# Conv and attention hybrid, tokens stage: another place in the turn for every kind of piece

## The chip, the cores and the metric

The kernel runs on one core of a Trainium2 chip. The metric is the time of one execution on the device in microseconds (us). The core has a matmul engine (TensorE, PE in the profile), a vector engine (VectorE, DVE), a scalar engine (ScalarE, ACT), GpSimd (POOL) and SyncE (SP), which here issues all of the tokens stage's transfers. Each engine executes its own list of instructions strictly in order; a wait at the head of a list holds up everything behind it. 

## The reference

Input x has shape (32, 96, 56, 56), that is 32 images of 96 channels and 3136 tokens. Cut to what matters:

```python
x = conv3(relu(bn(dwconv(relu(bn(conv1(x))))))) ; x = bn(x) + x_in     # layer 0
t = tokens(x)                                                          # (32, 3136, 96)
h = relu(bn(layernorm(t) @ w1.T))                                      # 192 hidden
X = fft(h, axis=tokens)
xr = relu(X.real * rd - X.imag * idg + rb); xi = relu(X.imag * rd + X.real * idg + ib)
t = t + bn(ifft(xr + 1j * xi).real @ w2.T)
t = t + ffn(layernorm(t))          # 96 -> 384 -> 96, operands rounded to an 8-bit float, sums to 16 bit
```

## The kernel before

Layer 0 takes the first half of the time: its own phases (conv, projection) leave their result for each image in a scratch tensor in HBM. The tokens stage (`tokens_stage`) does the rest, and the change lies wholly in it.

Work of the tokens stage on one image is cut into 40 kinds of pieces, 349 pieces in all. On TensorE: `mean1`, `square1` (sums of layernorm 1, 2 pieces each), `w1` (14), `stage1` (first half of the transform, 14), `spectrum` (second half, 6), `w2` and `stage3` (8 each), `stage4` (7), `mean2`, `square2`, `spread_mean`, `spread_rstd`, `mlp1` (21), `mlp2` (7). The other engines' pieces stand between them: for instance ACT's `act_mean1` (L1504), DVE's `dve_var1` (L1635), ACT's `act_std1` (L1471), and SP's `row1` (L1182), which copies the row of standard deviations with four small transfers into the tile `y`, where `w1` (L1386) takes it as an added row. 

The stage runs as a software pipeline over "turns". A turn has NT = 2000 slots, and `PLACES` gives each piece a place: place % 2000 is its slot in the turn, and place // 2000 is its lag, that is how many images behind the newest one it works. With 32 images and LAGS = 5 there are 36 turns. Every engine walks the slots of a turn in order (`tensor_turn`, `scalar_turn`, `vector_turn`, `pool_turn`, `sync_turn`) and issues its pieces that stand in the slot; pieces of one slot follow in the order in which the function lists them. The slot numbers of different engines are tied by nothing but the semaphores that the pieces wait on: only the order on each engine counts.

Resources that tie pieces together:
- Seven tiles of PSUM. `bank_w` (w1), `bank_s` (stage1), `bank_c` (w2 and stage3) and `bank_o` (stage4 and mlp2) are one bank each and in one copy, so the next piece on it waits until the one before is evacuated: `stage4` c waits for `dve_residual` c-1, `mlp2` c for `act_o` c-1, `w2` u for `dve_c` u-1. `bank_x` (spectrum) is in one copy as well: the next group waits for `dve_real` of the group before. `bank_l0` and `bank_l1` serve both layernorms, the spreads and mlp1.
- One queue of transfers. SP issues `load_in`, `row1`, `store_t`, `store_a`, `load_b`, `store_c`, `load_d`, `load_t`, `store_out` in the order of their slots. The transforms' two transposes go through HBM: `store_a` then `load_b` (L1215, L1192), `store_c` then `load_d` (L1197, L1204). `load_b` k=0 waits for all seven `store_a`; `load_d` k waits for `store_c` k to have landed. `store_c` k waits for `dve_c` of groups 2k and 2k+1. `load_t` brings back the residual tokens of the attention half, chunk by chunk, once `pool_out` has freed the chunk in the tile `tb`; `dve_residual` 0 waits for the first six chunks of `load_t`, `dve_residual` 6 for the last.

In the rows below and in the text, "X k" means the piece k of kind X. The two waits spoken of most are these:

```python
        if c == 0:
            dve.wait_ge(ld_t, (b + 1) * 16 * (NCH - 1))     # residual_vector, L1681
```

```python
        sp.wait_ge(st_c[k % 2], m * 32 + (k // 2 + 1) * 16)  # load_d, L1200
```

Of the kernel before, what the change touches and what calls it, by code (L numbers as in the profile page):

```python
# [100 lines left out]
def build(nc, x4, cw1, g1, b1, cw2, g2, b2, cw3, g3, b3, aw1, bn1g, bn1b, bn1m, bn1v, ar, ai, arb, aib,  # L101
# [13 lines left out]
    with keep:  # L115
# [881 lines left out]
        with st:  # L997
# [3 lines left out]

NT = 2000
LAGS = 5
PLACES = {'load_in': (0, 143, 286, 429, 571, 714, 863),
 'act_bn3': (341, 496, 576, 750, 888, 1052, 1183),
 'pool_y': (362, 517, 597, 771, 909, 1074, 1204),
 'store_t': (1247,),
 'act_square1': (1683, 2129),
 'mean1': (2073, 2154),
 'square1': (2092, 2169),  # L1010
 'act_mean1': (2117, 2210),
 'dve_var1': (2135, 2289),
 'act_std1': (2171, 2329),
 'row1': (2189, 2347),
 'w1': (2289, 2391, 2443, 2495, 2569, 2775, 2860, 2933, 3060, 3116, 3234, 3309, 3398, 3460),
 'dve_rstd1': (2314, 2414, 2466, 2518, 2641, 2820, 2904, 3025, 3084, 3152, 3272, 3331, 3424, 3487),
 'act_h': (2356, 2422, 2474, 2533, 2650, 2830, 2915, 3040, 3098, 3161, 3290, 3367, 3438, 3521),
 'stage1': (2407, 2459, 2585, 2695, 2877, 2949, 3005, 3132, 3266, 3343, 3414, 3476, 3552, 3630),
 'act_a': (2435, 2487, 2634, 2719, 2904, 2973, 3029, 3174, 3313, 3380, 3450, 3533, 3576, 3654),
 'store_a': (2502, 2734, 2988, 3189, 3395, 3548, 3669),  # L1020
 'load_b': (3765, 3781, 3901, 4264),
 'spectrum': (3897, 4032, 4326, 4731, 5023, 5149),
 'act_scaled': (3948, 4079, 4377, 4797, 5068, 5221),
 'dve_real': (3995, 4159, 4417, 4835, 5110, 5433),
 'pool_imag': (3986, 4118, 4415, 4835, 5103, 5250),
 'act_relu': (4030, 4188, 4512, 4866, 5134, 5495),
 'dve_fold': (4058, 4242, 4649, 5041, 5247, 5516),
 'w2': (4511, 4821, 4966, 5189, 5507, 5690, 5795, 5969),
 'dve_wz': (4557, 4867, 5029, 5235, 5571, 5736, 5841, 5990),
 'stage3': (4678, 4894, 5097, 5289, 5594, 5754, 5864, 6007),  # L1030
 'dve_c': (4722, 4918, 5156, 5334, 5672, 5778, 5928, 6039),
 'store_c': (4934, 5351, 5795, 6048),
 'load_d': (5035, 5481, 6020, 6241),
 'load_t': (5469, 5531, 5706, 5743, 5963, 6068, 6230),
 'stage4': (6371, 6424, 6476, 6551, 6602, 6659, 6712),
 'dve_residual': (6397, 6449, 6501, 6576, 6627, 6684, 6737),
 'act_square2': (6595, 6766),
 'mean2': (6621, 6791),
 'square2': (6641, 6807),
 'act_mean2': (6666, 6843),  # L1040
 'dve_var2': (6698, 6879),
 'act_std2': (6728, 6928),
 'dve_rstd2': (6752, 6958),
 'spread_mean': (6911, 7324, 7611, 7881),
 'spread_rstd': (7077, 7379, 7671, 7959),
 'dve_centre': (6930, 6944, 7345, 7359, 7638, 7652, 7908),
 'dve_norm': (7094, 7137, 7396, 7410, 7688, 7708, 7976),
 'mlp1': (7177, 7183, 7228, 7250, 7260, 7283, 7431, 7437, 7493, 7501, 7546, 7569, 7729, 7735, 7771, 7777, 7834, 7840,
          7995, 8001, 8026),
 'act_h16': (7198, 7210, 7244, 7263, 7275, 7303, 7461, 7484, 7510, 7543, 7559, 7586, 7742, 7754, 7783, 7794, 7847,  # L1050
             7857, 8008, 8020, 8052),
 'dve_bias1': (7216, 7227, 7276, 7284, 7292, 7322, 7478, 7501, 7536, 7583, 7592, 7603, 7760, 7770, 7800, 7811, 7863,
               7873, 8030, 8042, 8086),
 'dve_relu1': (7300, 7373, 7549, 7616, 7820, 7887, 8100),
 'mlp2': (7361, 7443, 7576, 7647, 7847, 7941, 8127),
 'act_o': (7389, 7473, 7601, 7671, 7871, 7981, 8159),
 'dve_bias2': (7427, 7490, 7666, 7702, 7922, 8025, 8188),
 'pool_out': (7438, 7502, 7677, 7714, 7934, 8038, 8199),
 'store_out': (8253,)}


def tokens_stage(nc, st, NB, x, out, z3_d, t_d, a_d, c_d, t1_d, t4_d, g2_d, g3_d, mean_w, s3, w1a, w2p, w2q, w2shift,
# [75 lines left out]
    K_OF = ((0, 8), (8, 8), (16, 8), (24, 5))  # L1138
    at = PLACES

# [643 lines left out]
```

## Time and profile before

| what | value |
|---|---|
| median of 3 runs | 5547.3 us (5545.8 to 5562.97) |
| profiled execution, its span | 5552.4 us |
| PE busy over the span | 5133.1 us, 92% |
| DVE, ACT, POOL busy | 3671.1 (66%), 3485.6 (63%), 2530.7 us (46%) |
| the transfers of SP's queue, share of 16 DMA engines | 62.9% |

The tokens stage begins near 2640 us and ends with the span. A view's window is given in us from the span's start. Busy time of an engine is the time in which an instruction of it is running; for PE the ends are modelled, so a matmul that starts inside the tail of the one before costs only the distance from start to start. "Idle before" is the time in which the engine had nothing running just before an instruction, with the releaser: what ended that wait. PEclk is the granted clock of TensorE as a share of 2.4 GHz.

### The profile page before, as it was taken

The numbers are of one execution on the slowest core, as the hardware profiler recorded it, in microseconds if no ns is written. First come the engines' busy times: TensorE is split into PE (matmuls) and PEld (weight loads), VectorE is DVE, ScalarE is ACT, GpSimd is POOL, SyncE is SP. The second block draws the span as 40 slices with busy tenths as digits, with TensorE's granted clock in tenths as the row PEclk, the third lists the DMA queues.
The fourth block names the chain that finished last, engine by engine and source line by source line (L and its number), as shares of the span: only waits on it lengthen the run. The fifth ranks groups of instructions, "written<-read, shape, count | busy, mean of one in ns | idle before, by whom it ended". The sixth has DMA issues, their size and how long they took to land.

```text
span 5552.4 us, 146819 instructions
## 1 busy us (share of the span) xinstructions
PE 5133.1 (92%) x59604; PEld 3433.9 (62%) x59604; DVE 3671.1 (66%) x6406; ACT 3485.6 (63%) x5863; POOL 2530.7 (46%) x1476
## 2 busy tenths in 40 slices
PE   8999999999999899997689999999999999999986
PEld 8856666666666544443566666667666666666763
DVE  1166666666678657776167777777777777777765
ACT  4455555555555488885466667666666676666752
POOL 0067777777777566664223333333333333333321
PEclk9999999999999999998799999999999999999996
DMA  7656666666666699997455565655656556566541
GB/s 161 146 145 171 163 172 170 162 172 169 172 167 167 162 417 418 415 416 293 129 165 159 154 179 154 169 168 157 175 147 169 161 161 177 153 168 172 158 122 46
DMA packets 493787, 1041.31 MB, mean 188 GB/s; under 512 B 176464, under 2 KB 345232, under 8 KB 460112
## 3 DMA queue, kind: packets, MB, share of 16 engines
q1 hardware_dynamic: 493120, 1031.92, 62.9%
q8 instruction: 479, 7.85, 0.6%
q14 instruction: 188, 1.54, 0.1%
HBM read 552.39 MB, written 478.94 MB: 186 GB/s over the span
## 4 chain that ended last, share of the span: by engine, by line
PE 35%; ACT 5%; DMA 4%; issue 4%; DVE 3%; SPq 1%; POOL 1%; DVEq 0%; POOLq 0%; ACTq 0%
PE bank_w L1386 5%; PE bank_s L1395 5%; PE bank_x L1341 4%; PE bank_o L1366 4%; PE bank_l L1295 4%; PE bank_c L1349 2%; DMA bt<-a_scratch 2%; PE bank_c L1350 2%; PE bank_o L1377 2%; PE bank_x L1338 2%; PE bank_l L1322 2%; ACT h L1461 1%; PE bank_c L1356 1%; SPq L1182 1%; PE bank_l L1283 1%
## 5 line engine op out<-in xcount | busy, mean ns | idle before, releaser
L736 POOL TENSOR_TENSOR hlo<-h,hhi 128x1682 f16<-128x1682 f32 x288 | 976.9, 3392 | 456.4 <-DVE hhi L789 456.4
L749 DVE BATCH_NORM_STATS2 stats<-z 128x6 f32<-128x392 f32 x1152 | 597.2, 560 | 486.1 <-ACT z L690 476.3
L700 ACT ACTIVATE h<-c1ps,s 128x1512 f32<-128x1512 f32 x288 | 465.1, 1615 | 691.5 <-PE c1ps L628 691.5
L649 PE MATMUL dwps<-hhi,taps 64*64 64x392 f16 x13824 | 688.1, 330 | 1.9 <-issue 1.8
L649 PE MATMUL dwps<-hlo,taps 64*64 64x392 f16 x13824 | 681.3, 328 | 1.4 <-issue 1.2
L1580 POOL TENSOR_TENSOR y<-zin,x_tok 96x448 f32<-96x448 f32 x224 | 254.2, 1135 | 790.3 <-ACT zin L1536 790.2
L1596 POOL TENSOR_TENSOR onat<-tb,o 96x448 f32<-96x448 f32 x224 | 237.0, 1058 | 781.2 <-DVE o L1656 781.2
L894 ACT ACTIVATE z2m<-z2m,s 128x784 f32<-128x784 f32 x512 | 489.5, 1029 | 105.8 <-DMA z2m<-z_scratch 105.4
L1386 PE MATMUL bank_w<-w1a,y 97*112 97x193 f32 x1792 | 414.7, 356 | 134.6 <-DMA y<-va 101.2
L918 POOL TENSOR_TENSOR h_split<-z2m,h_split 128x1568 f16<-128x1568 f32 x128 | 405.1, 3165 | 266.4 <-DVE h_split L957 266.4
L649 PEld LDWEIGHTS dwps<-hlo,taps 64*64 64x64 f16 x13824 | 402.5, 106 | 183.3 <-issue 3.3
L649 PEld LDWEIGHTS dwps<-hhi,taps 64*64 64x64 f16 x13824 | 378.9, 106 | 177.1 <-issue 3.9
L1530 ACT ACTIVATE h<-bank_w,rt 112x192 f32<-112x192 f32 x896 | 326.3, 418 | 211.3 <-PE bank_s L1395 129.5
L1386 PEld LDWEIGHTS bank_w<-w1a,y 97*112 97x112 f32 x1792 | 290.3, 187 | 261.3 <-DMA y<-va 127.6
L1587 POOL TENSOR_TENSOR s_plus<-d_minus,imag_scaled 128x448 f32<-128x448 f32 (+1 forms) x192 | 233.5, 1216 | 457.6 <-ACT imag_scaled L1446 457.6
L1461 ACT ACTIVATE h<-bank_l 128x448 f16<-128x448 f32 x672 | 342.4, 546 | 148.7 <-PE bank_l L1322 145.5
L628 PE MATMUL c1ps<-xhi,t1h 96*32 96x504 f16 (+1 forms) x4608 | 402.8, 340 | 8.5 <-ACT h L704 4.3
L1395 PE MATMUL bank_s<-h,t1c 112*128 112x192 f32 x1792 | 386.3, 339 | 3.4 <-ACT a L1523 3.4
L1643 DVE TENSOR_SCALAR h<-h,fqb 128x448 f16<-128x448 f16 x672 | 303.1, 470 | 120.7 <-ACT h L1461 107.5
L930 PE MATMUL pps<-z2m,w3T 128*96 128x392 f32 x1024 | 362.5, 497 | 15.0 <-ACT z2m L894 15.0
L628 PE MATMUL c1ps<-xlo,t1h 96*32 96x504 f16 (+1 forms) x4608 | 364.5, 337 | 2.4 <-issue 2.4
L1349 PE MATMUL bank_c<-w2p,zp 128*112 128x96 f32 x1856 | 347.8, 270 | 12.4 <-DVE cc L1718 12.3
(224 smaller groups left out, 10941.6 us busy)
## 6 DMA issues: line engine op xcount, KB each, us to landing
z_scratch<-z SPq DMA_DIRECT2D x1152, 196.0 KB, 3.3
z2m<-z_scratch SPq DMA_DIRECT2D x64, 1960.0 KB, 15.8
z2m<-z_scratch SPq DMA_DIRECT2D x64, 1568.0 KB, 11.5
a_scratch<-a SPq DMA_DIRECT2D x224, 384.0 KB, 2.4
bt<-a_scratch SPq DMA_DIRECT2D x96, 672.0 KB, 7.4
c_scratch<-cc SPq DMA_DIRECT2D x128, 336.0 KB, 3.6
d<-c_scratch SPq DMA_DIRECT2D x128, 336.0 KB, 4.0
xa<-in_x_dram SPq DMA_DIRECT2D x32, 1176.0 KB, 7.3
```

Of the source, the lines that this page charges most:

```text
L628: ins = nc.tensor.matmul(c1[32 * q:32 * q + 32, k, 0:cols], t1h[:, 64 * u + 32 * g:64 * u + 32 * g + 32], part[:, m, rows, :], start=(part ...
L649: ins = nc.tensor.matmul(dw[64 * j:64 * j + 64, r, g, 0:QN], taps[half, u, da, dx, :, :].rearrange("p y c -> p (y c)"), part[half, s, a0:a ...
L700: nc.scalar.activation(to, src, ACT.Relu, bias=s1[:, 1, u:u + 1], scale=s1[:, 0, u:u + 1]).then_inc(h_ready, 1)
L736: nc.gpsimd.tensor_tensor(to, h, hi, ALU.subtract).then_inc(lo_ready, 1)
L749: nc.vector.bn_stats(stats[:, i, v, at:at + 6], z2[:, v % 3, g, r, :]).then_inc(s_stat, 1)
L894: nc.scalar.activation(v, v, ACT.Relu, bias=s2[:, 1, t:t + 1], scale=s2[:, 0, t:t + 1]).then_inc(h2_ready, 1)
L918: nc.gpsimd.tensor_tensor(lo, h32, hi, ALU.subtract).then_inc(lo_ready, 1)
L930: nc.tensor.matmul(banks[m], w3T[:, t, :], z2m[:, c // 2, 4 * m + t, cols], start=(t == 0), stop=False)
L1349: nc.tensor.matmul(o, zp[:, k1 // 8 % 2, k1 % 8, :], w2p[:, :], start=True, stop=False)
L1386: ins = nc.tensor.matmul(WB[0:TP, 0, e * (H + 1):(e + 1) * (H + 1)], y[:, par, 2 * g + e, :, :].rearrange("p a b -> p (a b)"), w1a[:, :], ...
L1395: ins = nc.tensor.matmul(SB[:, 0, e * H:e * H + H], t1c[:, 2 * g + e, :], h[:, g % 2, e * H:e * H + H], start=True, stop=True)
L1461: nc.scalar.activation(h16[:, c % 2, q, :], LL[k % 2][:, 0, 0:CH], ACT.Copy).then_inc(h16_done, 1)
```

## The change

Only `PLACES` is different. No piece is added or taken away, no wait, no buffer, and the number of turns stays 36. All 40 kinds get other slots, and some pieces another lag: `mean1`, `square1`, `w1` 0 and their chain move from the image one behind to the newest (into the end of the turn before); `mlp1` 19 and 20, `mlp2` 6 and their followers move from lag 4 to lag 3; only `pool_out` 6 and `store_out` stay at lag 4. What follows from it is the order of the pieces on each engine.

```diff
--- before.py
+++ after.py
@@ -1001,62 +1001,62 @@
 
 NT = 2000
 LAGS = 5
-PLACES = {'load_in': (0, 143, 286, 429, 571, 714, 863),
- 'act_bn3': (341, 496, 576, 750, 888, 1052, 1183),
- 'pool_y': (362, 517, 597, 771, 909, 1074, 1204),
- 'store_t': (1247,),
- 'act_square1': (1683, 2129),
- 'mean1': (2073, 2154),
- 'square1': (2092, 2169),
- 'act_mean1': (2117, 2210),
- 'dve_var1': (2135, 2289),
- 'act_std1': (2171, 2329),
- 'row1': (2189, 2347),
- 'w1': (2289, 2391, 2443, 2495, 2569, 2775, 2860, 2933, 3060, 3116, 3234, 3309, 3398, 3460),
- 'dve_rstd1': (2314, 2414, 2466, 2518, 2641, 2820, 2904, 3025, 3084, 3152, 3272, 3331, 3424, 3487),
- 'act_h': (2356, 2422, 2474, 2533, 2650, 2830, 2915, 3040, 3098, 3161, 3290, 3367, 3438, 3521),
- 'stage1': (2407, 2459, 2585, 2695, 2877, 2949, 3005, 3132, 3266, 3343, 3414, 3476, 3552, 3630),
- 'act_a': (2435, 2487, 2634, 2719, 2904, 2973, 3029, 3174, 3313, 3380, 3450, 3533, 3576, 3654),
- 'store_a': (2502, 2734, 2988, 3189, 3395, 3548, 3669),
- 'load_b': (3765, 3781, 3901, 4264),
- 'spectrum': (3897, 4032, 4326, 4731, 5023, 5149),
- 'act_scaled': (3948, 4079, 4377, 4797, 5068, 5221),
- 'dve_real': (3995, 4159, 4417, 4835, 5110, 5433),
- 'pool_imag': (3986, 4118, 4415, 4835, 5103, 5250),
- 'act_relu': (4030, 4188, 4512, 4866, 5134, 5495),
- 'dve_fold': (4058, 4242, 4649, 5041, 5247, 5516),
- 'w2': (4511, 4821, 4966, 5189, 5507, 5690, 5795, 5969),
- 'dve_wz': (4557, 4867, 5029, 5235, 5571, 5736, 5841, 5990),
- 'stage3': (4678, 4894, 5097, 5289, 5594, 5754, 5864, 6007),
- 'dve_c': (4722, 4918, 5156, 5334, 5672, 5778, 5928, 6039),
- 'store_c': (4934, 5351, 5795, 6048),
- 'load_d': (5035, 5481, 6020, 6241),
- 'load_t': (5469, 5531, 5706, 5743, 5963, 6068, 6230),
- 'stage4': (6371, 6424, 6476, 6551, 6602, 6659, 6712),
- 'dve_residual': (6397, 6449, 6501, 6576, 6627, 6684, 6737),
- 'act_square2': (6595, 6766),
- 'mean2': (6621, 6791),
- 'square2': (6641, 6807),
- 'act_mean2': (6666, 6843),
- 'dve_var2': (6698, 6879),
- 'act_std2': (6728, 6928),
- 'dve_rstd2': (6752, 6958),
- 'spread_mean': (6911, 7324, 7611, 7881),
- 'spread_rstd': (7077, 7379, 7671, 7959),
- 'dve_centre': (6930, 6944, 7345, 7359, 7638, 7652, 7908),
- 'dve_norm': (7094, 7137, 7396, 7410, 7688, 7708, 7976),
- 'mlp1': (7177, 7183, 7228, 7250, 7260, 7283, 7431, 7437, 7493, 7501, 7546, 7569, 7729, 7735, 7771, 7777, 7834, 7840,
-          7995, 8001, 8026),
- 'act_h16': (7198, 7210, 7244, 7263, 7275, 7303, 7461, 7484, 7510, 7543, 7559, 7586, 7742, 7754, 7783, 7794, 7847,
-             7857, 8008, 8020, 8052),
- 'dve_bias1': (7216, 7227, 7276, 7284, 7292, 7322, 7478, 7501, 7536, 7583, 7592, 7603, 7760, 7770, 7800, 7811, 7863,
-               7873, 8030, 8042, 8086),
- 'dve_relu1': (7300, 7373, 7549, 7616, 7820, 7887, 8100),
- 'mlp2': (7361, 7443, 7576, 7647, 7847, 7941, 8127),
- 'act_o': (7389, 7473, 7601, 7671, 7871, 7981, 8159),
- 'dve_bias2': (7427, 7490, 7666, 7702, 7922, 8025, 8188),
- 'pool_out': (7438, 7502, 7677, 7714, 7934, 8038, 8199),
- 'store_out': (8253,)}
+PLACES = {'load_in': (0, 90, 94, 207, 254, 415, 1063),
+ 'act_bn3': (23, 244, 317, 593, 804, 925, 1045),
+ 'pool_y': (286, 593, 608, 935, 972, 1073, 1494),
+ 'store_t': (1595,),
+ 'act_square1': (1496, 1906),
+ 'mean1': (1786, 1879),
+ 'square1': (1827, 1937),
+ 'act_mean1': (1846, 2055),
+ 'dve_var1': (1847, 2205),
+ 'act_std1': (1881, 2379),
+ 'row1': (1761, 2620),
+ 'w1': (1925, 2018, 2131, 2245, 2280, 2432, 2504, 2571, 2677, 2802, 2902, 3060, 3103, 3166),
+ 'dve_rstd1': (1991, 2045, 2079, 2199, 2239, 2377, 2510, 2584, 2669, 2698, 2853, 2923, 3024, 3183),
+ 'act_h': (1955, 2119, 2202, 2245, 2322, 2403, 2550, 2681, 2828, 2890, 3006, 3051, 3189, 3275),
+ 'stage1': (2099, 2135, 2250, 2362, 2477, 2524, 2645, 2701, 2818, 2989, 3077, 3105, 3186, 3259),
+ 'act_a': (2174, 2214, 2294, 2398, 2453, 2636, 2763, 2837, 2987, 3040, 3070, 3196, 3278, 3305),
+ 'store_a': (2380, 2635, 2685, 2779, 3137, 3210, 3434),
+ 'load_b': (3441, 3564, 3824, 3860),
+ 'spectrum': (3485, 3738, 3925, 4468, 4624, 4844),
+ 'act_scaled': (3561, 3817, 4179, 4483, 4742, 5040),
+ 'dve_real': (3678, 3894, 4322, 4525, 4694, 5006),
+ 'pool_imag': (3559, 3701, 4300, 4710, 4737, 5232),
+ 'act_relu': (3774, 3929, 4373, 4675, 5027, 5299),
+ 'dve_fold': (3836, 4007, 4378, 4597, 4993, 5275),
+ 'w2': (4200, 4483, 4661, 4969, 5128, 5292, 5409, 5492),
+ 'dve_wz': (4124, 4508, 4613, 4866, 5161, 5348, 5505, 5668),
+ 'stage3': (4269, 4567, 4759, 5002, 5262, 5368, 5453, 5537),
+ 'dve_c': (4215, 4559, 4705, 4905, 5307, 5385, 5591, 5699),
+ 'store_c': (4597, 5344, 5452, 5622),
+ 'load_d': (5385, 5576, 5640, 5721),
+ 'load_t': (5149, 5478, 5594, 5711, 5734, 6004, 6470),
+ 'stage4': (5968, 6119, 6142, 6232, 6292, 6369, 6464),
+ 'dve_residual': (6014, 6078, 6115, 6174, 6268, 6355, 6476),
+ 'act_square2': (6246, 6445),
+ 'mean2': (6317, 6505),
+ 'square2': (6370, 6506),
+ 'act_mean2': (6378, 6584),
+ 'dve_var2': (6396, 6572),
+ 'act_std2': (6444, 6683),
+ 'dve_rstd2': (6508, 6726),
+ 'spread_mean': (6634, 6971, 7207, 7452),
+ 'spread_rstd': (6675, 7056, 7282, 7489),
+ 'dve_centre': (6600, 6603, 6872, 6884, 7247, 7272, 7529),
+ 'dve_norm': (6663, 6693, 6913, 6940, 7317, 7318, 7650),
+ 'mlp1': (6774, 6778, 6811, 6834, 6928, 6934, 7087, 7097, 7109, 7120, 7147, 7150, 7312, 7359, 7364, 7375, 7393, 7402,
+          7549, 7606, 7719),
+ 'act_h16': (6843, 6880, 6886, 6904, 6932, 6948, 7141, 7173, 7207, 7208, 7223, 7245, 7341, 7372, 7383, 7396, 7419,
+             7425, 7577, 7656, 7719),
+ 'dve_bias1': (6771, 6778, 6786, 6815, 6895, 7055, 7088, 7119, 7120, 7162, 7236, 7291, 7356, 7412, 7435, 7501, 7536,
+               7635, 7711, 7761, 7834),
+ 'dve_relu1': (6902, 7075, 7211, 7354, 7454, 7701, 7843),
+ 'mlp2': (7062, 7273, 7290, 7377, 7700, 7841, 7856),
+ 'act_o': (7053, 7310, 7337, 7453, 7716, 7867, 7889),
+ 'dve_bias2': (7059, 7325, 7341, 7507, 7788, 7904, 7923),
+ 'pool_out': (7105, 7410, 7508, 7533, 7689, 7740, 8665),
+ 'store_out': (8561,)}
 
 
 def tokens_stage(nc, st, NB, x, out, z3_d, t_d, a_d, c_d, t1_d, t4_d, g2_d, g3_d, mean_w, s3, w1a, w2p, w2q, w2shift,
```

On SP the order of the pieces about the end of a turn becomes (lag in brackets): store_a 6 [1], load_b 0 [1], store_c 2 [2], load_t 1 [2], load_b 1 [1], load_d 1 [2], load_t 2 [2], store_t [0], store_c 3 [2], load_d 2 [2], load_t 3 [2], load_d 3 [2], load_t 4 [2], row1 0 [0], load_b 2 [1], load_b 3 [1], and in the next turn load_in 0 [0], load_t 5 [3], load_in 1 [0]. Before, it was store_a 6, load_t 2, load_t 3, load_b 0, load_b 1, store_c 2, load_b 2, load_t 4, and in the next turn load_in 0, load_d 2, store_c 3, load_t 5, load_in 1, row1 0, load_t 6, load_d 3, store_out, load_b 3; store_t stood a third of a turn earlier, between store_a 3 and store_c 1.

## Rows read from the trace of the kernel before

**Rows 1.** Windows, turn by turn: one of the middle, the last three.

```profile
core 0: us, PE busy (x) PEld busy (x) DVE busy (x) ACT busy (x) POOL busy (x), PEclk, DMA share, GB/s
...
4864.40:4949.80 85.40, 78.75 (x546) 57.28 (x546) 62.61 (x121) 58.66 (x115) 29.06 (x27) 0.96 0.58 165
...
5291.40:5376.90 85.50, 79.80 (x545) 58.44 (x544) 61.42 (x121) 53.08 (x107) 21.17 (x20) 0.94 0.45 127
5376.90:5463.50 86.60, 70.20 (x390) 47.69 (x390) 57.49 (x103) 33.47 (x57) 19.93 (x19) 0.74 0.23 63
5463.50:5552.40 88.90, 50.81 (x162) 19.73 (x160) 37.79 (x69) 22.47 (x40) 9.25 (x9) 0.55 0.15 45
```

**Rows 2.** Groups of PE in that middle turn: count, busy us, mean ns, idle before.

```profile
L1386 PE MATMUL bank_w<-w1a,y 97*112 97x193 f32 x56 | 12.8, 353 | 3.7 <-DMA y<-va 3.1 <-ACT h L1530 0.5
...
L1322 PE MATMUL bank_l<-yq,fq 96*128 96x448 fp8e5 x23 | 7.0, 352 | 1.7 <-ACT h L1461 0.9 <-DVE yq L1676 0.8
```

**Rows 3.** Timeline near the same turn's start: start, duration, instruction, idle before.

```profile
4868.01 0.94 PE L1270 MATMUL bank_l<-sq,mean_w 96*32 96x448 f32 x8
...
4869.10 0.55 ACT L1504 ACTIVATE m2a<-bank_l 128x448 f32<-128x448 f32 x1
...
4870.00 0.74 PE L1377 MATMUL bank_o<-hq,fq 128*96 128x448 fp8e5 x3 [1.05 <-issue]
...
4871.21 0.66 ACT L1471 ACTIVATE va<-va,epsc 128x448 f32<-128x448 f32 x1
...
4871.96 2.40 SPq L1182 DMA_DIRECT2D y<-va  x4
...
4875.48 1.63 PE L1386 MATMUL bank_w<-w1a,y 97*112 97x193 f32 x4 [3.11 <-DMA y<-va]
```

**Rows 4.** Windows about that wait: the clock.

```profile
4874.40:4881.30 6.90, 5.82 (x27) 5.78 (x28) 1.47 (x4) 2.70 (x6) 1.13 (x1) 0.51 0.86 251
4881.30:4890.00 8.70, 8.70 (x73) 8.70 (x72) 4.83 (x10) 6.53 (x14) 4.51 (x4) 1.00 0.74 214
```

**Rows 5.** Timeline at the same turn's end.

```profile
4934.40 0.92 PE L1395 MATMUL bank_s<-h,t1c 112*128 112x192 f32 x4
...
4935.35 0.49 ACT L1523 ACTIVATE a<-bank_s 128x384 f32<-128x384 f32 x1 [1.88 <-PE bank_s L1395]
...
4940.17 0.55 DVE L1718 COPY cc<-bank_c 112x384 f32<-112x384 f32 x1
```

**Rows 6.** Transfers issued in that turn: count, KB each, median us to landing.

```profile
bt<-a_scratch SPq DMA_DIRECT2D x3, 672.0 KB, 7.5
c_scratch<-cc SPq DMA_DIRECT2D x4, 336.0 KB, 4.6
tb<-t_scratch SPq DMA_DIRECT2D x7, 168.0 KB, 2.6
zin<-z_scratch SPq DMA_DIRECT2D x7, 168.0 KB, 3.9
x_tok<-in_x_dram SPq DMA_DIRECT2D x7, 168.0 KB, 3.0
...
t_scratch<-y SPq DMA_DIRECT2D x1, 1176.0 KB, 5.6
d<-c_scratch SPq DMA_DIRECT2D x3, 336.0 KB, 3.5
bt<-a_scratch SPq DMA_DIRECT2D x1, 420.0 KB, 9.3
y<-va SPq DMA_DIRECT2D x7, 1.8 KB, 1.7
```

**Rows 7.** Windows in which the queue is full; columns as in rows 1.

```profile
4939.80:4955.00 15.20, 13.42 (x106) 8.17 (x104) 11.62 (x25) 9.25 (x19) 4.80 (x5) 1.00 1.06 250
...
4875.60:4883.20 7.60, 7.60 (x41) 7.56 (x42) 2.55 (x7) 4.44 (x10) 1.86 (x2) 0.63 1.01 295
```

**Rows 8.** The transfer that brings load_t 4, issued at 4947.27: us to landing.

```profile
tb<-t_scratch SPq DMA_DIRECT2D x1, 168.0 KB, 6.8
```

## The prediction

> **What bounds the kernel now.** I read the windows turn by turn first. A full turn of the tokens stage takes 85.4 us, and in it PE is busy for 78.75, DVE for 62.6, ACT for 58.7; the queue of transfers stands at 0.58 [rows 1]. So TensorE sets the turn, and its idle 6.65 us (85.4 - 78.75) are what an order can win. The groups of PE say where they lie: 3.7 before the first `w1`, nearly all of it behind the copied row (`y<-va`), and 1.7 spread over `mlp1` [rows 2].
>
> The timeline shows the first of these as one chain. `square1` 0 starts at 4868.01; ACT squares the mean at 4869.10; `act_std1` runs 4871.21 to 4871.87; SP issues the four row transfers from 4871.96 for 2.40 us; `w1` 0 starts at 4875.48 [rows 3]. That is 7.5 us from `square1` to `w1`, 3.5 of them from the first issue, and PE has work for only part of it: it idles 3.11 us, and 1.05 before the `mlp2` in between.
>
> The wait has a second price. In the 6.9 us from 4874.4 the granted clock is 0.51, the lower level of 1.2 GHz, after PE idled; from 4881.3 it is 1.00 again [rows 4]. PE was busy for 5.82 us of it; at full clock this work takes about half, so some 2.9 us go to the clock. What PE really needs in a turn is then 85.4 - 6.65 - 2.9 = 75.9 us.
>
> **What the change removes.** No instruction comes or goes; only waits can. Layernorm 1 and `w1` 0 now stand in the end of the turn before: `square1` 0, `mlp2` 5 and 6, `mean1` 1, `spectrum` 2, `w1` 0. Between `square1` 0 and `w1` 0 there are thus 4.9 us of PE work (0.94 + 0.66 + 0.67 + 0.78 + 1.87, distances from start to start in the timeline, `square1` itself included; first row 4868.01 in [rows 3]) against the chain's 7.5. `mlp1` is interleaved otherwise, with about the same idle: `mlp1` 14 now follows 12 and 13 directly and waits 0.4, `stage3` 7 waits 0.55 behind `dve_norm` 6.
>
> Stages 2 and 3 of the turn (from `stage4` 1 to `stage1` 13) need 48.3 us of PE by the same distances, and I find 0.8 us of idle in them when I go through the waits piece by piece: each evacuation has other pieces' work on PE before its successor. The first part, from `stage1` 13 over the turn's boundary to `stage4` 1, needs 27.6. The question is what it takes.
>
> **What the change adds: a line of transfers before one wait.** I put the start of `stage1` 13 at 0.
> - `act_a` 13 ends 1.4 us later (4934.40 to 4935.84, [rows 5]), `store_a` 6 and `load_b` 0 follow and have landed by about 8; `spectrum` 0 needs them at 11.5. Covered.
> - Next on SP is `store_c` 2, which waits for `dve_c` 5. In the old order `dve_c` 5 starts 5.8 us after `stage1` 13 [rows 5]; in the new one `spread_rstd` 2, two `mlp2`, `w2` 5 and three `mlp1` stand before `stage3` 5 and the copy ends at about 7.9. SP blocks until then, so the line starts at 7.9.
> - From there to `load_t` 5 SP issues, with nothing that leaves room: store_c 2, load_t 1, load_b 1, load_d 1, load_t 2, store_t, store_c 3, load_d 2, load_t 3, load_d 3, load_t 4, row1 0, load_b 2, load_b 3, load_in 0, load_t 5. By the sizes [rows 6] that is 336 x 5 + 168 x 5 + 672 x 2 + 1176 + 420 + 336 + 7 = 5803 KB, 5.94 MB (`load_in` is two transfers of 168). Before, `store_t` (1176 KB) stood in a stretch of its own.
> - A full queue moves 250 GB/s where these small-row transfers stand (share 1.06) and 295 where the big store is among them [rows 7]. I take 250, since eight of the sixteen are the transposes' small rows: 23.8 us; the ends are 20.1 (295) and 27.6 (`store_t` alone, 1.204 MB in 5.6 us with its latency, 215 GB/s [rows 6]).
> - To it come 1.7 us from the last byte to landing (a lone 168 KB chunk takes 2.6 [rows 6], of which 0.7 are bytes), and about 2 us of holes: `load_d` 3 waits for `store_c` 3 to land while only two transfers are behind it, and the four row issues hold SP for 2.40 [rows 3] while only two are left in the queue. This 2 is an estimate; bounds 0 and 3.
> - So `load_t` 5 lands at 7.9 + 23.8 + 1.7 + 2.0 = 35.4. That later transfers wait for all earlier ones is plain from `load_t` 4, which takes 6.8 us behind `load_b` 1, `store_c` 2 and `load_b` 2 [rows 8] where its like take 2.6.
>
> `dve_residual` 0 waits for that landing as nearly the first piece of DVE's turn; behind it are queued `dve_rstd1` 1, so `act_h` 1 and `w1` 2, and `stage4` 1, which needs the bank that it evacuates. It takes 0.7, so `stage4` 1 starts at 36.2. PE alone, with the waits on other engines (0.4 + 0.55, 0.3 for `spectrum` 1 behind `dve_real` 0, 1.0 for `mlp2` 6 behind `act_o` 5, which stands behind `act_scaled` 1 and `act_mean1` 0, 0.4 for `spectrum` 2) would be there at 30.3, and with 1.4 more for the row at `w1` 0 at 31.7. Nothing in the order hides the remaining 4.5.
>
> The Trainium skill ("DMA: Bandwidth & Descriptors", Queues, rings and completion order) says that completion is not in order of issue for a small transfer that uses few of the rings. By that the row could land ahead of what stands before it and `w1` 0 lose its 1.4 us. The sum stays, since `load_t` 5 is no such transfer and sets the same 36.2.
>
> **The sum.** Turn after: 48.3 + 0.8 + 36.2 = 85.3, plus the clock. The new order has two waits of some us close together (before `w1` 0 and before `stage4` 1), of which the low clock after the first falls partly under the second; I take 2.0 of the 2.9. Turn 87.3, against 85.4: +1.9. The boundary has all its transfers in 29 turns (those in which lags 0, 1 and 3 are live together): +55 us.
>
> The drain gets shorter. From `w1` 0 of the last image, 11.1 us into the third last window, it now takes 85.5 - 11.1 + 86.6 + 88.9 = 249.9 us [rows 1]. Moved by the pieces that went from lag 4 to 3 and from lag 1 to 0, the last image needs one turn of 85, one of 75 and a last of 78: 238, -12. These are bounded by nothing (no gain) and -25. Sum: 5552.4 + 55 - 12 in the profiled execution, +43; the median of the runs lies 5 us under the span, so 5547.3 + 43 = 5590.
>
> **The rivals.**
> 1. *The line of transfers is covered.* If the queue runs at 295 and without holes, `load_t` 5 lands at 29.7, before PE gets there at 31.7. Turn 48.3 + 0.8 + 31.7 + 1.5 (clock after one short wait) = 82.3, -3.1: 29 x -3.1 - 12 = -102, 5445. For it: 295 is in the trace; the old order has 0.42 of the queue free. Against: 250 holds where the same transfers stand. It decides from a landing before 31. Chance 0.25.
> 2. *They even out.* The line lands 1.5 us earlier than I take it, so that wait added and waits removed are alike: turn 85.8, +12 - 12: 5547. Chance 0.18.
> 3. *A second place where SP stands.* In the new turn `load_t` 6 waits for `pool_out` 6, behind two `pool_y`; after it come `store_c` 0 (waits for `dve_c` 1), `row1` 1 and `store_a` 1, which `w1` 8 and `stage1` 7 need. By my walk they arrive 2.0 and 1.2 us ahead of need. If SP is 4 us late there, PE loses about 3 more per turn: 5590 + 87 = 5677. It decides from a delay of 1.2 us. Chance 0.12.
>
> The forecast keeps 0.45.
>
> **How the numbers follow.** 5590. Its own range ends where rival 2 begins, at about 5550; with both upper bounds (queue 27.6, holes 3) the turn is 4.8 us longer, 5729, so I end it at 5690. The range for 8 in 10 takes in rival 1 and rival 3 at their prices and most of that upper end: 5440 to 5720. A measurement of this kernel can tell about 0.3% (17 us) from no change. Slower by more: the upper seven eighths of the forecast's 0.45 and rival 3, 0.52. Within: rival 2 less a little that falls to either side, 0.18. Faster by more: rival 1 and the low edge of rival 2, 0.30.
>
> **What would show it.** In the profile after, `stage4` 1 or `dve_residual` 0 (tb, L1686) must wait in each turn for a transfer (`tb<-t_scratch`), several us, and the queue's share must be near 1 from before the turn's boundary to that wait. The idle before `w1` (L1386) on the row should fall from 3.1 to about 1.4. `mlp2` 6 should wait 1.0 for `act_o` 5. If L1686 waits for no transfer, rival 1 holds. If `bank_s` or `bank_w` pieces in the middle of the turn wait for `a_scratch` or `y<-va`, it is rival 3. The prediction is wrong altogether if PE idles in places that I called covered, since each was judged with means of one execution.

## The result and the profile after

| | before | after |
|---|---|---|
| median | 5548.95 us (5545.8 to 5562.97) | 5606.45 us (5593.51 to 5612.36) |
| span of the profiled execution | 5552.4 us | 5602.4 us |
| ratio | | 1.0085, 95% interval 1.006 to 1.011 |

The medians are of four runs each. The new order is slower: the medians lie 57 us apart, the spans of the profiled executions 50. The predicted time was 5590.

The windows of the kernel after, of two neighbouring turns of the middle and the last three (columns as in [rows 1]):

```profile
4839.10:4924.60 85.50, 80.09 (x547) 58.31 (x546) 62.17 (x120) 59.05 (x115) 29.09 (x26) 0.95 0.54 159
4924.60:5015.50 90.90, 81.88 (x546) 59.66 (x545) 62.16 (x120) 59.30 (x115) 29.06 (x26) 0.93 0.56 161
5372.80:5454.90 82.10, 73.13 (x515) 55.72 (x513) 61.79 (x118) 51.26 (x104) 27.06 (x22) 0.96 0.47 128
5454.90:5529.90 75.00, 65.55 (x341) 42.19 (x341) 52.59 (x94) 28.33 (x49) 13.53 (x14) 0.73 0.27 72
5529.90:5602.40 72.50, 46.54 (x146) 17.36 (x146) 36.02 (x61) 20.11 (x36) 8.37 (x7) 0.55 0.10 33
```

Images are counted from 0. In the timeline of after `w1` 1 of image 2 starts at 2783.31 and that of image 31 at 5372.84, so 29 turns take 89.3 us each; before, the same two start at 2809.45 and 5308.31, 86.2 each. Most turns of before are alike: 23 of the 29 take 84.7 to 85.8 us, and six take 86.5 to 92.4. Those of after swing between 84.1 and 95.4. The turns bring +90 us. The head of the stage, up to `w1` 1 of image 2, is 26 us shorter. The end, from `w1` 1 of the last image on, goes from 5552.4 - 5308.3 = 244.1 to 5602.4 - 5372.8 = 229.6 us, -14. Together that is the 50 us between the spans.

The groups of PE over 2300 us of the middle, after first (columns as in [rows 2]):

```profile
L1386 PE MATMUL bank_w<-w1a,y 97*112 97x193 f32 x1440 | 337.6, 361 | 47.2 <-DMA y<-va 47.2
L1395 PE MATMUL bank_s<-h,t1c 112*128 112x192 f32 x1442 | 327.4, 352 | 33.6 <-ACT a L1523 33.3
...
L1366 PE MATMUL bank_o<-t4c,d 128*96 128x112 f32 x1420 | 206.2, 298 | 65.5 <-DVE tb L1686 65.5
...
L1377 PE MATMUL bank_o<-hq,fq 128*96 128x448 fp8e5 x546 | 157.1, 402 | 18.8 <-ACT o L1466 18.8
```

and before, the same stretch:

```profile
L1386 PE MATMUL bank_w<-w1a,y 97*112 97x193 f32 x1500 | 338.6, 350 | 99.8 <-DMA y<-va 84.2 <-ACT h L1530 14.4
L1395 PE MATMUL bank_s<-h,t1c 112*128 112x192 f32 x1504 | 316.9, 333 | 0.0
...
L1366 PE MATMUL bank_o<-t4c,d 128*96 128x112 f32 x1495 | 190.0, 273 | 0.5 <-DMA d<-c_scratch 0.3
```

The wait for the row falls from 84.2 to 47.2 us, as meant. In its place stand 65.5 us behind `tb` and 33.3 behind `a`. The first is this wait of DVE, with the transfer that ends it; the second view is of a single issue of `load_t` 5 and its time to landing:

```profile
DVE tb L1686 <- DMA tb<-t_scratch: 137.1, 29, 6.4
```

```profile
tb<-t_scratch SPq DMA_DIRECT2D x1, 168.0 KB, 6.4
```

In the timeline of the turn from 4839.1 on SP and the engines come to it like this:

```profile
4905.29 0.42 SPq L1219 DMA_DIRECT2D t_scratch<-y  x1
...
4917.75 0.67 ACT L1471 ACTIVATE va<-va,epsc 128x448 f32<-128x448 f32 x1 [0.56 <-DVE va L1637]
4918.51 2.40 SPq L1182 DMA_DIRECT2D y<-va  x4
...
4921.02 1.11 SPq L1192 DMA_DIRECT2D bt<-a_scratch  x2
...
4923.26 0.35 SPq L1211 DMA_DIRECT2D tb<-t_scratch  x1
...
4929.69 0.68 DVE L1686 SCALAR_TENSOR_TENSOR tb<-bank_o,w2shift,tb 96x448 f32<-96x448 f32 x1 [5.38 <-DMA tb<-t_scratch]
4930.42 1.81 PE L1366 MATMUL bank_o<-t4c,d 128*96 128x112 f32 x8 [4.37 <-DVE tb L1686]
```

SP issues the row 0.09 us after `act_std1` ends (4917.75 + 0.67 = 4918.42). It isn't held up by the queue; it waits for ACT. Then the two `load_b` are issued, then `load_in` 0, then `load_t` 5, which needs 6.4 us behind them. PE waits 4.37 us for it here.

The windows of the same stretch, from `store_c` 2 to the row, over the row, and from there to the landing of `load_t` 5, show where the queue runs dry (the last two columns are the share of the DMA engines and GB/s):

```profile
4902.00:4918.50 16.50, 15.32 (x111) 9.26 (x110) 13.64 (x28) 11.20 (x19) 6.99 (x7) 0.90 0.90 241
4918.50:4922.00 3.50, 2.47 (x22) 1.86 (x16) 0.89 (x3) 2.40 (x3) 1.28 (x2) 1.00 0.41 100
4922.00:4929.70 7.70, 4.04 (x26) 2.77 (x26) 1.34 (x4) 1.35 (x3) 0.00 (x0) 1.00 0.99 253
```

The granted clock over 2900:5200, before, then after, bears on the rest:

```profile
2900.00:5200.00 2300.00, 2116.70 (x14540) 1535.09 (x14538) 1674.70 (x3208) 1569.14 (x3077) 769.77 (x692) 0.96 0.57 163
```

```profile
2900.00:5200.00 2300.00, 2101.01 (x14000) 1527.00 (x13999) 1595.52 (x3097) 1523.27 (x2963) 773.25 (x670) 0.93 0.55 159
```

A mean of 0.96 of two levels, 1.0 and 0.5, is about 8% of the stretch at 1.2 GHz, and 0.93 about 14%. The clock's records in the two traces, added up, give 195 and 331 us. PE is busy nearly as long as before (2101 against 2117 us) and has done 540 fewer matmuls in it. So idle is not most of what the turn lost: 183 us before, 199 after. The same work takes longer. Part of that need not be the clock: the tail of a matmul with nothing behind it counts as busy in full.

### The profile page after: what moved, and what is told of

It is laid out like the page before. It is cut to its first block, busy times and chain, and to the rows that moved or that the text cites. A ratio compares the mean times of both kernels' runs of the same rounds, so it can differ in the third digit from the quotient of the medians.

```text
span 5602.4 us, 146819 instructions
## 1 busy us (share of the span) xinstructions
PE 5182.9 (93%) x59604; PEld 3471.7 (62%) x59604; DVE 3657.9 (65%) x6406; ACT 3498.6 (62%) x5863; POOL 2565.5 (46%) x1476
## 4 chain that ended last, share of the span: by engine, by line
PE 36%; DMA 7%; DVE 3%; SPq 3%; ACT 2%; issue 2%; POOL 0%; DVEq 0%; POOLq 0%; ACTq 0%
PE bank_s L1395 5%; PE bank_w L1386 5%; PE bank_l L1295 4%; DMA tb<-t_scratch 4%; PE bank_o L1366 3%; PE bank_c L1349 3%; PE bank_c L1350 3%; PE bank_c L1356 3%; PE bank_x L1341 3%; PE bank_l L1322 2%; PE bank_o L1377 2%; DMA c_scratch<-cc 2%; SPq L1182 1%; PE bank_x L1338 1%; PE bank_l L1283 1%
## 5 line engine op out<-in xcount | busy, mean ns | idle before, releaser
L1596 POOL TENSOR_TENSOR onat<-tb,o 96x448 f32<-96x448 f32 x224 | 292.0, 1304 | 761.4 <-DVE o L1656 761.4
L1580 POOL TENSOR_TENSOR y<-zin,x_tok 96x448 f32<-96x448 f32 x224 | 269.7, 1208 | 623.4 <-ACT zin L1536 623.2
L894 ACT ACTIVATE z2m<-z2m,s 128x784 f32<-128x784 f32 x512 | 489.5, 1029 | 100.4 <-DMA z2m<-z_scratch 100.0
L1587 POOL TENSOR_TENSOR s_plus<-d_minus,imag_scaled 128x448 f32<-128x448 f32 (+1 forms) x192 | 205.8, 1072 | 663.3 <-ACT imag_scaled L1446 663.3
L1395 PE MATMUL bank_s<-h,t1c 112*128 112x192 f32 x1792 | 405.4, 351 | 43.6 <-ACT a L1523 43.1
L1395 PEld LDWEIGHTS bank_s<-h,t1c 112*128 112x128 f32 x1792 | 316.9, 202 | 159.2 <-ACT h L1530 123.3
L1386 PEld LDWEIGHTS bank_w<-w1a,y 97*112 97x112 f32 x1792 | 307.8, 193 | 172.7 <-DMA y<-va 66.9
L1686 DVE SCALAR_TENSOR_TENSOR tb<-bank_o,w2shift,tb 96x448 f32<-96x448 f32 x224 | 152.2, 679 | 317.9 <-PE bank_o L1366 160.3
```

Source lines behind the costliest of these rows:

```text
L894: nc.scalar.activation(v, v, ACT.Relu, bias=s2[:, 1, t:t + 1], scale=s2[:, 0, t:t + 1]).then_inc(h2_ready, 1)
L1386: ins = nc.tensor.matmul(WB[0:TP, 0, e * (H + 1):(e + 1) * (H + 1)], y[:, par, 2 * g + e, :, :].rearrange("p a b -> p (a b)"), w1a[:, :], ...
L1395: ins = nc.tensor.matmul(SB[:, 0, e * H:e * H + H], t1c[:, 2 * g + e, :], h[:, g % 2, e * H:e * H + H], start=True, stop=True)
```

## The experiments

The theory after the first look: `load_t` 5 lands too late, behind a line of transfers; PE waits for it, and its clock falls about each wait. The rivals: small waits between engines and not the transfers; the row; a clock that costs nothing.

**e1: the store out of the line.**

```diff
- 'store_t': (1595,),
+ 'store_t': (2110,),
```

> The new order with one place changed: store_t goes from slot 1595 of its turn (inside the line of transfers before load_t 5) to slot 110 of the next, behind load_t 5 and load_in 2. The line loses 1176 KB. My theory (the line sets the boundary): load_t 5 lands 4.8 us earlier, the wait of dve_residual 0 (L1686) for a transfer, 137 us over turns 4 to 31 in the new order's trace, falls under 30, the idle of PE that hangs on it (bank_o behind tb, 65 us) under 15, and some of the low clock goes with it: 5606 - 65 - 20 = about 5520. Rival A (the line is waited for, but PE is bound by small waits between engines and the clock, and a new wait takes its place): the time stays within 15 us of 5606. Rival B (the row is what counts, not load_t 5): the wait before w1 0 falls too, from about 2 us to 0 in each turn, and the time falls to 5480.

5607.2 us, ratio to before 1.0099 (1.0078 to 1.0121): no change from after. Its waits over 2900:5200:

```profile
DVE tb L1686 <- DMA tb<-t_scratch: 131.4, 27, 6.6
...
PE bank_o L1366 <- DVE tb L1686: 77.4, 25, 6.0
```

The 1176 KB are gone from the line and the wait is what it was. So the line does not act as one sum from `store_c` 2 on, as the prediction had it. What stands ahead of the row has landed before the row's last transfer, 1.0 us before it on the median in after and 3.3 in e1, and the row is issued when ACT is done. That leaves what stands between the row and `load_t` 5, which the next run moves. My expectation of 5520 failed; rival A's number fits, but not its reason, as the next run shows.

**e2: the two big loads behind load_t 5.**

```diff
- 'load_b': (3441, 3564, 3824, 3860),
+ 'load_b': (3441, 3564, 4010, 4015),
```

> The new order with two places changed: load_b 2 and 3 (1092 KB) go behind load_t 5, from slots 1824 and 1860 to slots 10 and 15 of the next turn; store_t stays in the line. The row (row1 0) stands before both places and is not helped. My theory: load_t 5 lands 4.5 us earlier, L1686 waits under 30 us in all for transfers, the wait before w1 0 keeps its 2 us a turn; about 5525, like the other move. Rival A: within 15 us of 5606. If a move of the store helps and this one does not, it was the row or the store and not the landing of load_t 5.

5485.4 us, 0.9877 (0.9858 to 0.9895): 121 us faster than after, and faster than before.

```profile
DVE tb L1686 <- DMA tb<-t_scratch: 9.0, 8, 1.7
...
PE bank_o L1366 <- DVE tb L1686: 1.4, 3, 0.7
```

This settles it: 1092 KB between the row and `load_t` 5 are the wait. From the first issue of the row to the landing of `load_t` 5 it takes a median of 11.8 us in after, 11.6 in e1 and 7.4 in e2 (turns 4 to 31 of each trace). The wait goes from 65.5 to 1.4 us on PE in 2300 us, some 2.5 us in each of 29 turns, 72 us. The gain is 121. The rest goes with the clock, of which 259 us instead of 331 are at the lower level in the 2300, and with the tails of matmuls that had waited less than a tail is long; the two I can't separate.

**e3: the mirror in the old order.**

```diff
- 'store_t': (1247,),
+ 'store_t': (1790,),
```

> The old order with store_t moved from slot 1247 into its own line of transfers, between load_b 1 and store_c 2 (slot 1790): the mirror of the first run. In the old order the row is issued 7.6 us after mlp1 19 and the transfer before it has landed at 8.2, the row at 11.1. My theory: the line grows by 4.8 us, the row lands about 2.6 us later, in each of 30 turns, so 5549 + 78 = about 5627, the idle before w1 rising from 3.1 to 5.7 us a turn. Rival (a transfer's place costs nothing while the queue is free 42% of the time): within 15 us of 5549.

5580.9 us, 1.0051 (1.0033 to 1.0069): slower by 27, between my 78 and the rival's 15. The idle before `w1` rises less than I said:

```profile
L1386 PE MATMUL bank_w<-w1a,y 97*112 97x193 f32 x1492 | 343.3, 355 | 116.1 <-DMA y<-va 100.4 <-ACT h L1530 14.5
```

It is 100.4 against 84.2 us: 0.6 us a turn more, where I expected 2.6. It is the same mistake as in e1: most of the store's 4.8 us did not reach the row. My reading, which no run tests by itself, is that a place in the queue costs what is left of it when the next small transfer is needed.

**e4: one small DVE piece.**

```diff
- 'dve_rstd1': (..., 3024, 3183),
+ 'dve_rstd1': (..., 3024, 3121),
```

> The new order with one small place changed on DVE: dve_rstd1 13 goes ahead of dve_wz 4 and dve_bias1 9 (slot 1183 to 1121). In the new order's turns PE idles 1.1 us before stage1 13, behind act_a 12, which stands on ACT behind act_h 13, which waits for dve_rstd1 13. No transfer is touched. Theory of the line: stage1 13 comes 0.6 us earlier, and with it all that follows to the line, so up to 0.6 x 28 = 17 us, and the wait for load_t 5 keeps its length: 5590 to 5606. Rival (small waits and the clock that they bring carry the loss): 17 us of idle and at least as much in clock, under 5575.

5559.7 us, 1.0013 (0.9998 to 1.0028): 47 us faster than after, for one reciprocal moved ahead of a copy and a bias.

```profile
L1395 PE MATMUL bank_s<-h,t1c 112*128 112x192 f32 x1464 | 334.3, 353 | 15.2 <-ACT a L1523 15.1
...
L1366 PE MATMUL bank_o<-t4c,d 128*96 128x112 f32 x1456 | 211.1, 298 | 76.8 <-DVE tb L1686 76.8
```

The wait for `a` falls from 33.3 to 15.1 us. The wait for `tb` grows from 65.5 to 76.8, and another, of the spectrum for DVE, from 5.8 to 16.0. So PE's idle as a whole is what it was: 199 us of the 2300 in after, 198 in e4. What fell is the busy time of the same work: 2102 us for 14215 matmuls, against 2101 for 14000 (the traced executions, 5569.5 and 5604.2, lie 35 us apart and not 47).

My theory gave at most 17 us, the rival under 5575: the rival is right. In the records of the clock of after, 68 us of low clock in turns 4 to 31 begin between 48 and 64 us after `w1` 1, that is about and behind this wait; in e4 there are 3. Over the 2300 us the low clock falls from 331 to 283. That the gain is the clock fits these figures, but it isn't measured apart from the tails.

**e5, e9: the moves together.** e9 has e2's and e4's edits, e5 those and e1's.

> The new order with two moves: load_b 2 and 3 behind load_t 5, and dve_rstd1 13 ahead of dve_wz 4; store_t stays in the line. It separates store_t in the three moves together (5409). If store_t costs nothing where load_t 5 isn't waited for, 5405 to 5415. If it fills the queue in front of spectrum 1 or load_t 5 once the rest is faster, 5430 to 5440, with the wait of L1686 for transfers above its 21 us.

> The new order with the three moves together: load_b 2 and 3 behind load_t 5, store_t behind load_in 2, dve_rstd1 13 ahead of dve_wz 4. Alone they gave -121, 0 and -47 us. If two waits at different places of the turn were removed, the gains add: 5606 - 121 - 47 = about 5440. If they shared one cause (the clock's state over the whole turn), they overlap: 5470 to 5490.

e9: 5430.6 us, 0.9782 (0.9745 to 0.9818). e5: 5408.9 us, 0.9744 (0.9724 to 0.9763). The two gains add: -121 - 47 = -168, measured -176 in e9. In e5 it is -197, 31 us more than I expected. `store_t`'s place, worth nothing in e1, looks worth about 20 us here, but the runs of e9 spread from 5408 to 5439, and its wait for `tb` is no longer than e5's (14.6 and 20.9 us over 2900:5200), so the reason given for it isn't borne out. Why it helps stays open.

**e8, e12: another small wait.**

```diff
- 'mlp1': (..., 7359, 7364, 7375, ...),
+ 'mlp1': (..., 7359, 7370, 7375, ...),
```

> The new order with load_b 2 and 3 behind load_t 5, dve_rstd1 13 ahead of dve_wz 4, and mlp1 14 behind stage3 5 instead of ahead of it, so that its wait for act_h16 12 (0.54 us a turn) has a matmul in it. By the waits alone -0.3 x 29 = -9 us against the two moves (5440), about 5430; if a short wait costs its clock too, up to -25 more.

> The three moves (5409) and mlp1 14 behind stage3 5, the last move of e8 put on top of them. If that move is worth its 0.3 us a turn, about 5400; if it is what made e8 slower than the three moves, 5420 to 5440.

e8, on top of e9's 5430.6: 5435.4 us. e12, on top of e5: 5405.8 us (0.9743, 0.9724 to 0.9762, against 0.9744). No effect that can be told apart. Not every half microsecond of idle has a price.

**e6, e7, e10, e11: matmuls that nobody reads, in the waits.** Nothing of the computation is left out; in a wait PE does five more matmuls on `y` and `w1a` into the bank that `w1` 0 will overwrite. For that the wait for the evacuation of this bank stands ahead of them, and so ahead of the one for the row (the call is shortened here):

```diff
+        for e in range(FILL if g == 0 else 0):                # FILL = 5
+            nc.tensor.matmul(WB[0:TP, 0, 0:H + 1], y[0:C, par, 0, :, :]..., w1a[0:C, :], start=True, stop=True)
         if g in (0, 8):
             pe.wait_ge(ld_row, ...)
```

e6 has after's places and also ten matmuls on `d` and `t4c` before `stage4` 1, into `bank_c` and behind a wait for its last evacuation; e7 stands on e9, e10 on e5, e11 on before.

> The new order with matmuls added whose results nobody reads: five (ten passes, 1.6 us) before w1 0 waits for the row, ten (twenty passes, 1.9 us) before stage4 1 waits for dve_residual 0. No wait is removed, no place is changed. Theory (the waits cost a second time through the granted clock): the stretches at 1.2 GHz about the turn's boundary (212 us of the 419 in turns 4 to 31 of the new order's trace begin there) nearly vanish, and with PE busy through most of them, half of that comes back: 5606 - 100 + 10 for fillers that overrun = about 5515. Rival (the clock falls for another reason, or costs only time that PE would wait anyway): 5600 to 5640.

> The new order with load_b 2 and 3 behind load_t 5, dve_rstd1 13 ahead of dve_wz 4, and the five unread matmuls before w1 0 alone. The wait for the row (1.6 us a turn) stays, the low clock after it should go (some 78 us of low clock begin there in the trace with the moved load_b). If the clock theory holds: 5440 - 35 = about 5405. If not, the time of the moves alone or up to 20 us more.

> The three moves and the five unread matmuls before w1 0. By the clock theory the low stretches that begin after the wait for the row go, and the time falls from 5409 to about 5390. If the filler only shifts work, 5405 to 5425.

> The old order, nothing moved, with the five unread matmuls (1.6 us) before w1 0 waits for the row. In the old order's trace PE idles 3.1 us there in each turn and the clock is at 1.2 GHz for 3.4 to 6.8 us from about that wait on, 174 of the 195 us of low clock between 2900 and 5200. Theory (the idle lowers the clock and the clock costs half of its stretch): the low stretches there go, 5550 - 29 x 2.5 = about 5478. Rival (the wait's length alone counts): 5550, since the wait ends with the row in both.

| | base | with fillers | ratio to before | clock over 2900:5200, base and with |
|---|---|---|---|---|
| e6, on after | 5606.5 | 5580.0 | 1.006 (1.0037 to 1.0083) | 0.93, 0.96 |
| e7, on e9 | 5430.6 | 5406.5 | 0.9736 (0.9716 to 0.9756) | 0.96, 0.98 |
| e10, on e5 | 5408.9 | 5383.8 | 0.9712 (0.9684 to 0.974) | 0.97, 0.98 |
| e11, on before | 5550.4 | 5553.7 | 1.0007 (0.9994 to 1.002) | 0.96, 0.97 |

The window of e10, the fastest kernel here, 3% under before:

```profile
2900.00:5200.00 2300.00, 2206.03 (x15584) 1619.57 (x15582) 1752.89 (x3385) 1656.76 (x3237) 842.71 (x725) 0.98 0.60 171
```

The fillers raise the clock in every case, so idle lowers it. They bring about 25 us three times, where I expected 35 of e7, 19 of e10 and some 90 of e6. In the old order, where I expected 72, they bring nothing. e11's groups of PE show where it goes, first those of before, then those of e11:

```profile
L1341 PE MATMUL bank_x<-g2c,bt 112*128 112x112 f32 x1534 | 229.4, 312 | 8.3 <-DMA bt<-a_scratch 8.1
...
L1338 PE MATMUL bank_x<-g2c,bt 112*64 112x112 f32 x1588 | 94.3, 274 | 0.0
```

```profile
L1390 PE MATMUL bank_w<-w1a,y 97*112 97x193 f32 x1512 | 329.2, 340 | 60.4 <-DMA y<-va 45.2 <-ACT h L1534 14.0
...
L1342 PE MATMUL bank_x<-g2c,bt 112*128 112x112 f32 x1550 | 198.8, 282 | 8.9 <-DMA bt<-a_scratch 8.7
L1367 PE MATMUL bank_o<-t4c,d 128*96 128x112 f32 x1512 | 183.9, 265 | 18.0 <-DMA d<-c_scratch 18.0
...
L1339 PE MATMUL bank_x<-g2c,bt 112*64 112x112 f32 x1588 | 111.1, 305 | 0.1
...
L1385 PE MATMUL bank_w<-w1a,y 96*112 96x193 f32 x260 | 49.1, 336 | 0.0
```

The spectrum's matmuls of 128 columns take 282 ns where they took 312, those of 64 columns 305 where they took 274: the low stretches are fewer (120 us instead of 195 over the 2300), and some have moved. Without the 49.1 us of the fillers PE is busy for 2096 us, 21 less than before. But it now comes to `stage4` 0 too early and waits 18.0 us for `load_d` (0.3 before), and 11.2 for DVE's `va` (3.2 before). So by these rows what the clock gives back in this order is waited away: there PE's own work does not set what comes next.

## Why the prediction was right, and where it wasn't

**That it gets slower, by a new wait at stage4 1 for load_t 5.** Right, and shown by e2. The marks of the turn of the timeline above, from the start of `stage1` 13 at 4893.8: `store_c` 2 issued at 8.2 (forecast 7.9), `load_t` 5 landed at 35.9 (35.4), `stage4` 1 at 36.6 (36.2). The sign named for it holds but for the row: the queue's share is 0.90 and 0.99, with 3.5 us of 0.41 between.

**The full line of 5803 KB.** Wrong, though it gave the right landing, and that was luck. This is the step that failed: I let the sixteen transfers run as one line from `store_c` 2, with 2.0 us of holes, and found 35.4. e1 takes a fifth of the bytes out and nothing moves. The break is at the row: SP issues it when `act_std1` ends, and everything behind it counts from there. The right sum starts at the issue of the row (4918.51) and has three terms: 2.4 us for its four transfers, 6.5 for 1596 KB at 250 GB/s and 1.7 for the landing. That gives 10.6; in the traced turn `load_t` 5 landed 11.2 us behind the row's issue (4923.26 + 6.4 = 4929.66). The two sums come out alike because in this order the queue had drained (`load_t` 4 landed) 1.0 us before the row's last transfer did. The 1.7 is a small slip of its own: 2.6 less 0.7 is 1.9.

**Its size on PE.** 4.5 us a turn forecast; 2.5 on the mean (65.5 us over 26 waits, the longest 5.3). The wait is shorter where PE itself comes late; what makes it late in a turn no run separates. The row: 1.4 forecast, 1.9 on the mean (47.2 over 25). `mlp2` 6 behind `act_o` 5: 1.0 forecast, 0.7 (18.8 over 26). PE's idle in all: forecast +2.8 a turn (9.4, which is 85.3 less the 75.9 of work, against 6.65), measured 183 us in 26.7 turns and 199 in 25.8: +0.9 a turn.

**The clock.** The mis-sized term. I took 2.0 us a turn, less than the 2.9 of before. By the clock's records the low clock grew from 195 to 331 us in 2300, 7.3 to 12.8 us a turn. If PE loses half of it, an estimate, that is +2.8 where I had -0.9. The busy time of a turn, which takes in the clock and the tails, grew by less: 2117 us in 26.7 turns, 2101 in 25.8, +2.2. With the 0.9 of idle that is the 3.1 us by which the turn became longer, against the forecast 1.9. So idle was taken 1.9 too high and the clock some 3 too low, and the two errors partly cancel.

**The waits that I called covered.** One was missed: `stage1` 13 behind `act_a` 12, 33.3 us over 2300. I had only 0.8 us of idle in all between `stage4` 1 and `stage1` 13; the reciprocal `dve_rstd1` 13 stands behind a copy and a bias on DVE. The move that halves this wait was worth 47 us (e4), four fifths of the difference between the two kernels.

**The end and the head.** The end, from `w1` 0 of the last image: 249.9 to 238 forecast, -12; it starts at 5368.03 in after, so 234.4 measured, -15.5. The head, -26, I had not worked out: the first image's `w1` begins a turn earlier. The 5590 is near for this reason too: the turns brought +90 us and not +55, and the head took most of the difference back. I also took 85.4 us for every turn of before, where the mean of 29 is 86.2.

**The rivals.** Rival 1 (the line is covered) is false for after and true for e2. Rival 3's place shows in the trace as 41.2 us in which `act_a` waits for a store, but PE doesn't wait there: `stage1` loses 0.2 us outside the `stage1` 13 case. The row of `w1` 0 gained nothing by landing out of turn: in the traced turn `w1` 0 starts 3.5 us after the first issue, as before, and the last of the four transfers landed behind `load_t` 4 in all of 29 turns. By the Trainium skill ("DMA: Bandwidth & Descriptors", Queues, rings and completion order) a small transfer that uses few of the rings need not land in the order of issue. The trace of before agrees, for another row: of `row1` 1 the first transfer, issued at 4880.61, took 4.2 us, and the `load_in` issued ahead of it at 4878.30 took 7.9, so the row landed 1.4 us ahead.

## What to carry to other kernels

In a queue of transfers in order, look for the last one that is issued late for its own reasons, here the row behind ACT, and count the bytes between it and the transfer that an engine waits for; what stood ahead of it here was free (1176 KB, e1). Loads that are needed half a turn later don't belong between them: moving two of them was worth 121 us of 5606.

## What the hardware showed that I had not expected

- A wait of PE of 1.3 us in each turn (33.3 us in 25.8 turns), cut to about half, gave 47 us over 29 turns, 1.6 us a turn, though PE's idle in all stayed the same (e4). The low clock fell from 331 to 283 us in 2300.
- Fillers of 1.9 us in a wait (49.1 us for 260 matmuls, ten a turn) raised the clock (0.96 to 0.97 in the old order) and brought nothing there, and gave 25 us of 5409 in the order in which PE's work set the pace.
- The row, four transfers of 1.8 KB, holds SP for 2.40 us in both orders, nearly as long as a lone 168 KB chunk takes to land (2.6, [rows 6]).
- A 1.8 KB transfer landed 1.4 us ahead of one of 168 KB that SP had issued 2.3 us before it (trace of before).
